# A fused adaLN layer on one core: order of the first head group's maxima, folds, gate steps and rotations

## The reference

```python
mod = (_silu(c) @ wmod).reshape(1, 6, 1, -1)              # sa, ca, ga, sb, cb, gb
ga, gb = sign * max(abs, 0.25)
h = _layernorm(x) * (1 + ca) + sa
# attention: 32 heads, 64 plain + 64 rotary query columns, latent keys and values of 32
q = _rmsnorm(h @ wq_a.T, q_a_ln_w) @ wq_b.T               # rotary columns de-interleaved and rotated
ckv, k_pe = split(h @ wkv_a.T); kv = _rmsnorm(ckv, w) @ wkv_b.T
attn = softmax(causal(q_full @ k_full.T * scale)) @ v
x = x + ga * (attn @ wo.T)
h = _layernorm(x) * (1 + cb) + sb
x = x + gb * down(silu(gate(h)) * up(h))                  # int32 weights with scales, I = 1376
```

## Time and profile before

| | |
|---|---|
| median of three runs | 753.69 us |
| profiled execution | 753.28 us |
| its span | 751.5 us |
| TensorE busy | 719.4 us (96%) |
| VectorE busy | 543.3 us (72%) |
| ScalarE busy | 327.2 us (44%) |
| GpSimd busy | 215.5 us (29%) |
| granted TensorE clock | 0.999 |

### The profile page before, as it was taken

The page is one execution under the profiler, slowest core; times in us unless marked ns, Lnnn a source line. Parts: engine busy times, 40 slices in busy tenths (PEclk is TensorE's granted clock), DMA queues, the critical chain, the costliest instruction groups (busy, mean ns, idle before and its releaser), DMA issues.

```text
span 751.5 us, 10449 instructions
## 1 busy us (share of the span) xinstructions
PE 719.4 (96%) x3829; PEld 503.8 (67%) x3829; DVE 543.3 (72%) x802; ACT 327.2 (44%) x499; POOL 215.5 (29%) x197
## 2 busy tenths in 40 slices
PE   3889999999999999999999999999999999999997
PEld 2866566666666666666666666555788888887886
DVE  6878689799799799799799789686893323213432
ACT  4844555545545545555555454445254322222210
POOL 1149535145145145145145020100463000000211
PEclk9999999999999999999999999999999999999999
DMA  8934633403403403403403480440210432200101
GB/s 322 253 84 114 143 72 85 103 1 85 103 0 85 103 1 85 103 1 85 103 0 85 117 333 2 168 169 1 84 29 1 126 84 63 58 10 1 41 31 43
DMA packets 40211, 63.43 MB, mean 84 GB/s; under 512 B 4512, under 2 KB 20896, under 8 KB 38304
## 3 DMA queue, kind: packets, MB, share of 16 engines
q1 hardware_dynamic: 40160, 62.75, 30.6%
HBM read 32.99 MB, written 2.10 MB: 47 GB/s over the span
## 4 chain that ended last, share of the span: by engine, by line
PE 72%; DVE 21%; issue 3%; ACT 1%; POOL 1%; DMA 1%; SPq 0%; DVEq 0%; POOLq 0%; ACTq 0%
PE PS L980 16%; PE PS L804 9%; PE PS L997 8%; PE PS L885 7%; PE PS L867 7%; PE PS L874 6%; PE PS L870 6%; DVE PR L1532 5%; PE PS L944 5%; DVE NMa L1442 3%; DVE wide L1532 3%; PE PS L795 3%; PE PS L817 2%; DVE NMd L1447 1%; PE PS L825 1%
## 5 line engine op out<-in xcount | busy, mean ns | idle before, releaser
L1192 ACT ACTIVATE PR<-PS 128x1024 f32<-128x1024 f32 (+1 forms) x144 | 133.2, 930 | 137.2 <-PE PS L874 106.1
L804 PE MATMUL PS<-KH,Q 96*128 96x128 f32 (+3 forms) x576 | 133.3, 330 | 9.3 <-DVE TQ L1434 3.6
L1442 DVE TENSOR_REDUCE NMa<-PS 128x1 f32<-128x512 f32 (+3 forms) x184 | 117.6, 658 | 25.1 <-PE PS L804 22.8
L804 PEld LDWEIGHTS PS<-KH,Q 96*128 96x128 f32 x576 | 87.7, 190 | 65.0 <-issue 32.4
L867 PE MATMUL PS<-Q,KH 96*128 96x512 f32 x288 | 118.6, 412 | 0.0
L1532 DVE TENSOR_TENSOR PR<-PR 128x2048 f32<-128x2048 f32 (+3 forms) x56 | 114.3, 2041 | 3.6 <-ACT PR L1192 1.2
L874 PE MATMUL PS<-Q,KH 97*128 97x512 f32 (+1 forms) x288 | 114.2, 396 | 0.3 <-DMA Q<-NM 0.3
L870 PE MATMUL PS<-Q,KL 96*128 96x512 f32 (+1 forms) x288 | 113.5, 394 | 0.0
L1780 POOL TENSOR_SCALAR_AFFINE_SELECT diag<-diag 128x512 f32<-128x512 f32 x64 | 44.6, 696 | 187.1 <-ACT diag L1135 186.9
L867 PEld LDWEIGHTS PS<-Q,KH 96*128 96x128 f32 x288 | 54.6, 190 | 27.6 <-issue 14.3
L885 PE MATMUL PS<-PR,V 128*32 128x512 f32 (+3 forms) x704 | 70.2, 486 | 0.0
(11 more groups left out here) (192 smaller groups left out, 1080.7 us busy)
## 6 DMA issues: line engine op xcount, KB each, us to landing
Q<-TQ SPq DMA_DIRECT2D x56, 384.0 KB, 5.6
RT<-in_wo SPq DMA_DIRECT2D x4, 1024.0 KB, 4.8
TQ<-in_wo SPq DMA_DIRECT2D x4, 1024.0 KB, 5.0
Q<-TQ SPq DMA_DIRECT2D x16, 192.0 KB, 3.4
WI<-in_gate_w SPq DMA_DIRECT2D x10, 256.0 KB, 3.6
WI<-in_up_w SPq DMA_DIRECT2D x10, 256.0 KB, 4.1
DI<-in_down_w SPq DMA_DIRECT2D x10, 256.0 KB, 2.7
PR<-in_wmod_c SPq DMA_DIRECT2D x2, 1024.0 KB, 6.3
```

Of the source, the lines that this page charges most:

```text
L804: ins = pe.matmul(bank[:, i * w:(i + 1) * w], M.Q[0:KR, g % 2, 0, qt // 4, h0 + i, qs], M.KH[0:KR, lo:lo + w], start=(i == 0), stop=(i == ...
L1192: act.activation(tiles, banks, ACT.Exp).then_inc(S_.p, 1)
L1442: dve.tensor_reduce(dst, PS[:, bank_of(turn), 0:n * w].rearrange("p (h k) -> p h k", k=w), axis=AX.X, op=ALU.max, negate=True).then_inc(S_ ...
```

## The change

It rewrites the list of the stage. Behind the three products of group 0's second half, the list now begins with the first maxima part. The low part of the latents stands behind part 0 as before; the fold of group 1's weights moves from ahead of part 0 to behind part 2. The key "split", 0, 1 moves behind part 3, and the GpSimd share of it becomes a key of its own, "rest", 0, 1, behind part 7. The third gate step moves from ahead of part 0 to behind part 4, the fourth from behind part 5 to behind part 6, the first gate's copy from behind part 7 to behind part 8. Group 1's "even", "odd", "lat" with "sum", and "split" of the first half move behind the diagonal parts of one tile further. "low", 1, 0 moves from behind part 14 to behind part 19. The three dummies ahead of part 0 move behind part 2. On GpSimd the keys "even", 1, 1 and "odd", 1, 1 do nothing any more, and "sum", 1, 1 does their four products before its two sums. No computation is added or left out.

```diff
@@ -463,21 +463,20 @@
 TABLES = [window_table(w) for w in range(G)]
 FIRST_FOLDS = [("w", 0)]
 FIRST_QUERIES = [[(kind, 0, hf) for kind in ("even", "odd", "lat", "low", "split")] for hf in range(2)]
-FIRST_QUERIES[1].remove(("low", 0, 1))
-FIRST_QUERIES[1].insert(3, ("w", 1))
+FIRST_QUERIES[1] = FIRST_QUERIES[1][0:3]
 
 MOD_STEPS = [("modstep", 0, n, k) for n in range(2) for k in range(KD)]
 
 INPUT_STEPS = {2: FIRST_FOLDS, NS - 3: FIRST_QUERIES[0][0:2], NS - 2: FIRST_QUERIES[0][2:5],
                NS - 1: [("rest", 0, 0)] + MOD_STEPS[0:1], NS: MOD_STEPS[1:2]}
 
-FIRST_MAXIMA = MOD_STEPS[2:3]
-MOD_PIECES = dict(zip((5, 10, 14, 18, 21), ([step] for step in MOD_STEPS[3:])))
-MOD_PIECES.update({7: [("modrow", 0, 0)], 26: [("modrow", 0, 1)]})
-
-LOW_PIECES = {0: [("low", 0, 1)], 14: [("low", 1, 0)], len(PARTS) - 1: [("lat", 1, 1)]}
-
-HANDED_PIECES = {0: [("even", 1, 0)], 1: [("odd", 1, 0)], 2: [("lat", 1, 0), ("sum", 1, 0)], 3: [("split", 1, 0)],
+FIRST_MAXIMA = []
+MOD_PIECES = dict(zip((4, 6, 10, 14, 18, 21), ([step] for step in MOD_STEPS[2:])))
+MOD_PIECES.update({8: [("modrow", 0, 0)], 26: [("modrow", 0, 1)]})
+
+LOW_PIECES = {0: [("low", 0, 1)], 2: [("w", 1)], 3: [("split", 0, 1)], 7: [("rest", 0, 1)], 19: [("low", 1, 0)], len(PARTS) - 1: [("lat", 1, 1)]}
+
+HANDED_PIECES = {1: [("even", 1, 0)], 2: [("odd", 1, 0)], 3: [("lat", 1, 0), ("sum", 1, 0)], 4: [("split", 1, 0)],
                  5: [("even", 1, 1)], 6: [("odd", 1, 1)], 7: [("sum", 1, 1)]}
 for key in [key for _, key, _ in sorted(group_places(0, maxima_places(0.0, 0.9)), key=lambda x: x[0])]:
     FIRST_MAXIMA.append(key)
@@ -906,11 +905,11 @@
         side(key)
     pe.wait_ge(S_.cr, NS)
     for key in FIRST_MAXIMA:
-        if key == ("part", 0, 0):
-            keep_busy(2, 3)
         if key == ("rows", 0):
             keep_busy(2, 5)
         side(key)
+        if key == ("part", 0, 2):
+            keep_busy(2, 3)
         if key[0] == "part" and key[2] % 2 == 1 and key[2] not in MOD_PIECES:
             keep_busy(2, 2)
     keep_busy(2, 10)
@@ -1799,15 +1798,21 @@
             weights_low(g)
         elif kind == "part" and is_diagonal(key[2]):
             diagonal(g, key[2])
+        elif kind in ("even", "odd") and (g, key[2]) == (1, 1):
+
+            pass
         elif kind == "even" and g in HANDED:
             rotate_even(g, key[2])
         elif kind == "odd" and g in HANDED:
             rotate_odd(g, key[2])
         elif kind == "sum":
+            if key[2] == 1:
+                rotate_even(g, 1)
+                rotate_odd(g, 1)
             rotated_sum(g, key[2])
         elif kind == "odd" and (g, key[2]) != (0, 0):
             rotate(g, key[2])
-        elif kind == "rest" or kind == "split" and (g, key[2]) != (0, 0):
+        elif kind == "rest" or kind == "split" and g > 0:
             split_low(g, key[2])
         elif kind == "norm":
             normalise(g, key[2])
```

## The result

The changed kernel takes 756.76 us (median of six runs, 756.58 to 757.45), the kernel before 753.75 beside it: 3.0 us slower, a ratio of 1.0045 with a 95% interval of 1.0034 to 1.0055. The profiled execution took 756.91 us on a span of 755.1. The forecast was 755.5, on the right side, but 1.3 us short, and the measured time lies just outside its range.

What follows compares the result with a forecast made beforehand. TensorE was taken to bound the kernel. The late products' landing, 1.8 us late at part (1, 11), set the sum, with ScalarE's 1.0 inside it: 755.1 us profiled, 755.5 median, range 754.0 to 756.7.

Steps and rivals of the forecast that it cites:

- The products behind the last mask: GpSimd, second half of group 1: four products after the last diagonal mask finish the sums 4.35 us later; deciding term, +1.8.
- the landing before part (1, 11): Window 0: head 2's queries land at 97.85, so TensorE's part (1, 11), formerly at 96.05, waits 1.8 us.
- the sum: The forecast's total on the span: +1.8 us, giving 755.1 for a profiled execution and 755.5 for the median.
- ScalarE's queue: Before window 0: late split delays the copy for part (1, 5), slip 1.0, inside the 1.8; as deciding rival 754.7, chance 0.12.
- the two last waits: Window 0: TensorE waits before part (1, 5) for ScalarE's copy, then before part (1, 11) for a DMA at 97.8.
- The held join: VectorE's maxima join, blocked by GpSimd's products: rows 0.5 to 1.7 later, under the sends; as deciding rival 755.4, chance 0.10.
- the sends: SP's sends of half (1, 1): first issue at 89.91 against 86.37, deciding the time at 755.5, chance 0.50.
- TensorE's list is equal, so I carry 0.1 to the end.: Stage behind part 9: order changes but not the number of steps, so the opening's 0.1 us lag stays unchanged.
- Banks rotate by one name ..., the ring's order stays: nothing.: Bank rotation in all windows: the reordered list costs nothing through the banks.
- the dummies at 0.88: Opening: parts 5 and 7 get two dummies each, 4 x 0.22 = 0.88 us more on TensorE.
- balance of the opening: Opening on TensorE: 8.18 - 1.05 waits + 0.88 dummies + 0.28 wait at part 3 = 8.29 us, 0.1 later.
- one case of a larger slip, 756.3: Rival: joins holding GpSimd, late window masks, or TensorE's clock falling in longer idle time; +2.6, chance 0.10.

Runs made afterwards that it cites:

- e1: Kernel before the change with only GpSimd's four products of (1, 1) moved into the sum step, behind the last mask: 755.70 us against 753.44, ratio 1.0035.
- e9: Changed kernel with (odd, 1, 0) back behind part 8 and low part of (1, 0) behind part 17: 755.25 us, against 756.53 for the changed kernel.
- e7: Changed kernel with half (1, 1) sent in two passes, high parts before low parts: 755.54 us against 753.21 for the kernel before, ratio 1.0032.
- the repeat: The changed kernel timed and profiled again, nothing altered: 756.53 us against 753.58 for the kernel before, ratio 1.0035.
- e3: Changed kernel with the low part of the latents of (1, 0) behind part 17 instead of 19: 756.34 us.
- e5: Changed kernel without the four added dummies behind parts 5 and 7: 756.55 us beside 756.53 for the changed kernel.
- e10: As e11, but (lat, 1, 0) also ahead of part 9 and its low part behind part 10, four added dummies kept: 752.90 us, ratio 0.9997.
- e12: As e10, but without the four added dummies behind parts 5 and 7: 752.05 us, ratio 0.9983 to the kernel before.
- e11: Changed kernel keeping only early maxima: GpSimd's products in their steps, group 1's even and odd behind part 8, low behind 14: 752.98 us against 753.21.

## Why the prediction was wrong in size

**Right: the direction, the deciding term and its price.** The products behind the last mask were named as what decides, through ScalarE's split, GpSimd's rest, SP's sends and the landing before part (1, 11). The chain up to the first send grew by 3.58 (forecast 3.44), and the products cost 1.9 to 2.1 in seven profiles, where the sum has 1.8 less the 0.1 of the stage. By medians they cost 2.3 in e1 and 1.7 in e9. Part (1, 5), held by ScalarE's queue, is 2.47 late, of which 1.48 is the stage's: 0.99, forecast 1.0. e7 shows the order of the two last waits as forecast. The held join came as described and stayed under the sends; the rows are 1.89 late, 0.41 more than the stage.

**Wrong: "TensorE's list is equal, so I carry 0.1 to the end."** This is the step that failed: it priced the stage's lag at 0.1 us, and the stage ends 1.48 late in the first profile and 1.07 late in the repeat. Counting TensorE's work up to the product of (even, 1, 0) was near enough: 8.17 us (50.50 to 58.67) where the forecast had 8.29. But the next item in the list had changed. Before, (odd, 1, 0) stood there, 0.75 us that reached to part 9 at 59.31, just behind a landing that can't be moved: the second half's high parts hang on GpSimd's rotation, which the sum itself had said keeps its time. Now part 9 stands there, TensorE waits, and the product comes on top behind it. That is one half, up to 0.7 us (part 20 is 0.73 late), more or less by how the landing falls: the send is issued at the same distance from the first matmul, 7.26 to 7.28 us, in all profiles, and took 2.7 us to land in e3, 3.5 before the change, 3.7 in the changed kernel and 4.2 in e1. Why it varies, no run shows.

**Wrong: "Banks rotate by one name ..., the ring's order stays: nothing."** The order of the ring stays, but what holds a bank changed. (lat, 1, 0) keeps its bank until VectorE's low step. The product moved four parts back and the low step five, to behind part 19, while the ring comes round to that bank at part 21. Before, the ring came round to it at part 17, three parts behind the low step; now it is two. So TensorE waited for it, 0.54 us shown, and e3 takes the wait away and brings the last copy 0.72 earlier. e9 shows the two halves together: 1.3 by the medians, and a last copy that is on time (-0.09).

**Wrong in its working, and without effect: the dummies at 0.88.** Their added work is in the page, but it stands ahead of the landing and costs nothing there (0.02 in e5). The forecast's balance of the opening (a wait won, dummies lost) weighed two things that both end at the same landing. The early maxima bring nothing for the same reason, and by e11 they cost nothing that its interval (0.9987 to 1.0005) would show.

**The range.** It took 0.1 to 0.4 for the stage, bounds that came from how matmul ends are drawn, not from what else TensorE might meet. The rivals had one case of a larger slip, 756.3, which is near the measured time, but not for its reasons: TensorE's granted clock is 1.00 from 80.90 to 104.00 in the changed kernel as before, and no mask or join is the last wait there. That the measured time came close to this case is luck. The first half of group 1, (1, 0), is sent 3.0 later (74.07 instead of 71.08), not 2, and nothing in window 0 waits for it.

## What to carry to other kernels

When a list is reordered, equal work on the bounding engine isn't equal time: go through the new list and ask two things of each item at the time when it is now reached: has what it reads landed, and who still holds its bank? In this kernel an item just ahead of a landing that TensorE has to wait for was free, and the same item behind it cost in full. That held for a product of 0.75 us, and for four dummies, worth 0.02 in e5 and 0.85 between e10 and e12. Time won in front of the landing became a gain only when work from behind it was moved there, as in e12.

## What the runs showed that I had not expected

The join of 128x16 elements took 0.34 us before and 0.91 after; before the change its median over the windows was 0.176. In both cases it ended 0.03 us behind the end of a two-input operation of GpSimd (81.79 before, 83.82 after). The second join (83.88) then started 0.01 us ahead of GpSimd's next product, which took 1.31 us; the products ahead of it took 1.26 or 1.27. It is the same in all eight profiles with late products: a join of 0.91 or 0.92 and a next product of 1.30 or 1.31. In the six others the join took 0.33 to 0.35. So VectorE was held up for one operation of GpSimd and not for its whole run, and the rows came 0.41 later than the stage's own lag, under the 0.5 to 1.7 that I gave.
